# One list schedule for softmax attention, experts and the gated delta net: layer 0 from its router on joins layer 1's plan

## What is computed

```python
xn = layernorm(x)
s  = softmax_attention(xn)          # 16 heads of 16, causal, scores / 4
g  = silu(moe(xn))                  # 8 experts, top 2: silu(xn w1) * (xn w2), then w3
x  = x + s * g                      # layer 0
xn = layernorm(x)
s  = gated_delta_net(xn)            # 16 key heads, 32 value heads, conv of 4 taps
g  = silu(moe1(xn))                 # 2 shared experts, 16 routed, top 2, gelu
x  = x + s * g                      # layer 1
```

## Time and profile before

| what | us |
|---|---|
| median of 3 runs (lowest, highest) | 1588.99 (1585.53, 1592.14) |
| the profiled execution, its own time | 1583.53 |
| span of its trace | 1581.8 |
| PE busy, share of the span | 1443.0, 91% |
| DVE busy, share | 1244.6, 79% |
| ACT busy, share | 973.3, 62% |
| POOL busy, share | 650.3, 41% |

### The profile page before, as it was taken

The page is one execution under the profiler, slowest core; times in us unless marked ns, Lnnn a source line. Parts: engine busy times, 40 slices in busy tenths (PEclk is TensorE's granted clock), DMA queues, the critical chain, the costliest instruction groups (busy, mean ns, idle before and its releaser), DMA issues.

```text
span 1581.8 us, 33450 instructions
## 1 busy us (share of the span) xinstructions
PE 1443.0 (91%) x12600; PEld 1169.3 (74%) x12600; DVE 1244.6 (79%) x2613; ACT 973.3 (62%) x2525; POOL 650.3 (41%) x778
## 2 busy tenths in 40 slices
PE   6998778698899999989999999998999999999995
PEld 3554323386788888878878888887888888888883
DVE  3457624558888988979999888998989988898883
ACT  2100243238777677857777867776777777777763
POOL 7010032245545444445454444545354444443323
PEclk9999877769999999999999999999999999999997
DMA  9940000102111111111101111101021111011000
GB/s 289 115 53 4 4 0 1 40 21 52 34 28 35 35 28 28 41 28 35 35 28 35 35 35 28 48 21 48 8 55 28 31 32 35 22 37 32 9 1 27
DMA packets 52744, 59.37 MB, mean 38 GB/s; under 512 B 5352, under 2 KB 45032, under 8 KB 52584
## 3 DMA queue, kind: packets, MB, share of 16 engines
q1 hardware_dynamic: 52584, 57.23, 15.6%
HBM read 51.71 MB, written 5.51 MB: 36 GB/s over the span
## 4 chain that ended last, share of the span: by engine, by line
PE 67%; DVE 16%; POOL 5%; ACT 4%; issue 3%; DMA 3%; SPq 0%; POOLq 0%; DVEq 0%; ACTq 0%
PE ps L815 16%; PE ps L1155 6%; PE ps L867 4%; PE ps L1029 3%; PE ps L1133 3%; DVE O L1538 3%; PE ps L1137 3%; DMA RC<-crow 3%; PE ps L1109 3%; PE ps L1110 2%; PE ps L1071 2%; PE ps L1061 2%; PE ps L1125 2%; PE ps L1074 2%; DVE yv L1406 2%
## 5 line engine op out<-in xcount | busy, mean ns | idle before, releaser
L1724 ACT ACTIVATE XY<-ps 128x512 f16<-128x512 f32 x384 | 216.5, 598 | 103.9 <-PE ps L1074 102.8
L1471 DVE TENSOR_TENSOR ZL<-ps,cst 128x256 f16<-128x256 f32 x384 | 152.2, 416 | 26.9 <-PE ps L1061 24.8
L1866 POOL TENSOR_TENSOR RC<-RC,dec 128x512 f32<-128x512 f32 x64 | 67.0, 1047 | 232.8 <-DMA RC<-crow 232.7
L1406 DVE SCALAR_TENSOR_TENSOR yv<-ps,cw,yv 128x511 f32<-128x511 f32 (+2 forms) x192 | 142.9, 745 | 4.5
L1538 DVE SCALAR_TENSOR_TENSOR O<-O,small,Z 128x128 f32<-128x128 f32 x256 | 125.4, 550 | 9.5 <-POOL small L1897 9.5
L1155 PE MATMUL ps<-WO,OGT 128*128 128x256 f32 x512 | 127.8, 393 | 2.1 <-ACT OGT L1763 0.8
L1071 PE MATMUL ps<-ZL,XY 128*128 128x64 f16 x1536 | 103.9, 193 | 2.8 <-DVE ZL L1471 2.6
L1071 PEld LDWEIGHTS ps<-ZL,XY 128*128 128x128 f16 x1536 | 83.1, 98 | 30.2 <-issue 12.6
L1155 PEld LDWEIGHTS ps<-WO,OGT 128*128 128x128 f32 x512 | 94.0, 194 | 14.2 <-issue 1.1
L1074 PE MATMUL ps<-XY,ZL 128*128 128x64 f16 x1536 | 103.2, 193 | 0.0
L1061 PE MATMUL ps<-XY,LT 128*128 128x64 f16 x1536 | 96.8, 193 | 3.4 <-DVE yv L1406 1.1
(11 more groups left out here) (261 smaller groups left out, 4592.9 us busy)
## 6 DMA issues: line engine op xcount, KB each, us to landing
RC<-crow SPq DMA_DIRECT2D x128, 128.0 KB, 3.9
WV<-in_WV SPq DMA_DIRECT2D x16, 512.0 KB, 3.7
WK<-in_WK SPq DMA_DIRECT2D x16, 256.0 KB, 2.8
WO<-in_WO SPq DMA_DIRECT2D x16, 256.0 KB, 2.8
KS<-spread SPq DMA_DIRECT2D x6, 512.0 KB, 17.9
QS<-spread SPq DMA_DIRECT2D x6, 512.0 KB, 42.1
up<-in_up SPq DMA_DIRECT2D x18, 128.0 KB, 2.3
dn_w<-in_down SPq DMA_DIRECT2D x18, 128.0 KB, 2.4
```

The source lines that it names most:

```text
L1406: m = dve.scalar_tensor_tensor(out=dst[:, k:512], in0=ps[:, bk, 0:512 - k], scalar=cw[:, h, j, 3 - k:4 - k], in1=dst[:, k:512], op0=ALU.mu ...
L1471: leave(dve.tensor_tensor(half(ZL[:, k - 2], k, 0), p, lv(k), ALU.mult), "a", u, k)
L1724: leave(act.activation(changed(u, k), ps[:, bank("b", u, k), :].rearrange("p (c n t) -> p c n t", c=2, t=1 << (k - 1)), ACT.Copy), "b", u, k)
```

## The change

Layer 0 from the router on goes into the same plan as layer 1. `moe0`, `rows0`, the blend and both written orders are gone, and with them the barriers at `EXD_END`. Three new functions add the parts: `plan_experts0`, `plan_softmax0` and `plan_rows0`. `arrange` learns parts that take two neighbouring banks (`takes=2`). The arrival of QS and KS is a part on SP of 46 us (`stack`), the way of the maxima through DRAM one of 5 us (`max`).

The memory is laid out anew: w1 lies where XL comes later, and w2, w3, hT and the router's weights have room of their own beside PT and aT. So `ln1` (which writes XL) now comes after all expert products on PE, and nothing else in softmax waits for the experts but `op` on DVE, which needs the gate. The denominators are three items in place of one: `oc` (ACT), `ov` (PE, then DVE), `am` (POOL), each placed by itself. All eight XH copies of `ln1` are ACT's (before, DVE did four). What needs the new layernorm in layer 1 depends on `NEXT`, the last `ln1`. The numbers in `RANK` are other ones throughout, those of layer 1's parts too. No product, activation or DMA is added or left out.

```diff
--- before
+++ after
-ORDER_MOE0 = list(order_moe0())
-ORDER_SOFT0 = list(order_soft0())
...
+STEPS = [(b, g, j) for b in range(2) for g in range(4) for j in range(4)]
+STEP = {x: n for n, x in enumerate(STEPS)}
+PV_AT = {x: n + 1 for n, x in enumerate(x for x in STEPS if x[2] != 3)}
...
+            if p.takes == 2:
+                return min(((max(bank_at[b], bank_at[b + 1]), b) for b in spare if b % 2 == 0 and b + 1 in spare),
+                           default=None)
+            return min(((bank_at[b], b) for b in spare), default=None)
...
+def plan_experts0(P):
+    P.add(("rt",), -160, ("PE", 3.6), ("DVE", 0.3), takes=True, gives=("rt",))
+    P.add(("tp", 1), -160, ("DVE", 3.3, (("rt",), "DVE")), ("ACT", 1.5))
+    P.add(("tp", 2), -160, ("DVE", 3.0, (("tp", 1), "ACT")))
+    for k in range(16):
+        e, b = divmod(k, 2)
+        rank = -100 + 2 * k
+        old = [(("exd", *divmod(k - 3, 2), q), "PE") for q in range(2)] if k > 2 else []
+        x, y = ("exg", e, b), ("exv", e, b)
+        P.add(x, rank, ("PE", 1.72), ("ACT", 0.62, *old), takes=True, gives=x)
+        P.add(y, rank + 1, ("PE", 1.72), ("DVE", 0.69, (x, "ACT")), takes=True, gives=y)
+        for q in range(2):
+            z = "exd", e, b, q
+            P.add(z, rank + 2, ("PE", 0.86, (y, "DVE")), ("DVE", 0.96, (("exd", e - 1, b, q), "DVE") if e else (("tp", 2), "DVE")),
+                  takes=True, gives=z)
+    for b in range(2):
+        P.add(("g0", b), -60, ("ACT", 1.7, *[(("exd", 7, b, q), "DVE") for q in range(2)], (("g0", 0), "ACT") if b else None))
+
+
+def plan_softmax0(P):
+    P.add(("stack",), -300, ("SP", 46.0))
+    for b in range(2):
+        for g in range(8):
+            for i in range(4):
+                x = "p1", b, g, i
+                P.add(x, -200 + 20 * b, ("PE", 0.16 + 0.055 * (i + 1), (("stack",), "SP")),
+                      ("DVE", 0.1 + 0.27 * (i + 1)), takes=2, gives=x)
+        P.add(("tn0", b), -200 + 20 * b,
+              ("DVE", 0.7, *[(("p1", b, g, i), "DVE") for g in range(8) for i in range(4)], (("tn0", 0), "DVE") if b else None))
+        P.add(("tn", b), -200 + 20 * b, ("PE", 0.44, (("tn0", b), "DVE")), ("DVE", 0.68), takes=True, gives=("tn", b))
+        P.add(("max", b), -200 + 20 * b, ("SP", 5.0, (("tn", b), "DVE")))
+    for n, x in enumerate(STEPS):
+        b, g, j = x
+        part, no, rank = (4 - j) / 4, 4 * b + g, -190 + 80 * b + n % 16
+        back = STEPS[n - 3] if n > 2 else None
+        for k in range(2):
+            before = ("sc", *x, 0) if k else ("sc", *STEPS[n - 1], 1) if n else None
+            P.add(("sc", *x, k), rank, ("PE", 0.24 * part + 0.02, (("max", b), "SP"), before and (before, "PE")),
+                  ("ACT", 0.2 + 0.83 * part, back and (("pv", *back), "PE"), before and (before, "ACT")), takes=2,
+                  gives=("sc", *x, k))
+        last = ("pv", *STEPS[n - 1]) if n else None
+        P.add(("mk", *x), rank, ("POOL", 0.65, (("sc", *x, 0), "ACT"), (("sc", *x, 1), "ACT")))
+        P.add(("pv", *x), rank, ("PE", 0.86 * part + 0.05, (("mk", *x), "POOL"), last and (last, "PE")), takes=j == 0)
+        if j == 3:
+            am = (("am", *divmod(no - 2, 4)), "POOL") if no > 1 else None
+            P.add(("oc", b, g), rank, ("ACT", 0.62, (("pv", *x), "PE"), am), gives=("pv", b, g, 0))
+            P.add(("ov", b, g), rank, ("PE", 0.86, (("oc", b, g), "ACT")), ("DVE", 3.36, am), takes=True, gives=("ov", b, g))
+            P.add(("am", b, g), rank, ("POOL", 1.27, (("ov", b, g), "DVE")))
+
+
+def plan_rows0(P):
+    for n in range(NT):
+        b = n // 4
+        P.add(("op", n), -90 + 60 * b, ("PE", 1.72, *[(("am", b, g), "POOL") for g in range(4)]),
+              ("DVE", 1.2, (("g0", b), "ACT"), (("op", n - 1), "DVE") if n else None), takes=True, gives=("op", n))
+    for b in range(2):
+        P.add(("nrm", b), -90 + 60 * b, ("DVE", 2.0, *[(("op", n), "DVE") for n in range(4 * b, 4 * b + 4)],
+                                         (("nr2", 0), "DVE") if b else None), ("POOL", 1.3))
+        P.add(("nr2", b), -90 + 60 * b, ("DVE", 1.9, (("nrm", b), "POOL")))
+    experts = [((w, *divmod(k, 2)), "PE") for w in ("exg", "exv") for k in range(16)]
+    for n in range(NT):
+        b = n // 4
+        old = [(("ln1", n - 1), e) for e in ("PE", "ACT", "DVE")] if n else [None] * 3
+        P.add(("ln1", n), -90 + 60 * b, ("PE", 0.22, (("nr2", b), "DVE"), *experts, old[0]),
+              ("ACT", 0.4, old[1]), ("DVE", 0.42, old[2]), takes=True, gives=("ln1", n))
+    P.add(("spg",), -100, ("POOL", 1.0))
+    for h in range(2):
+        P.add(("fWK", h), -100, ("POOL", 1.9))
+    end = ("op", NT - 1), "DVE"
+    for h in range(2):
+        P.add(("fWV", h), -8 + 4 * h, ("SP", 4.5, end), ("POOL", 3.8))
+        P.add(("fWO", h), -6 + 4 * h, ("SP", 3.0, end), ("POOL", 0.7))
+        P.add(("fup", h), -7 + 4 * h, ("SP", 3.0, end), ("POOL", 1.0))
+    P.add(("cc", 1), -9, ("POOL", 0.6, end))
+    P.add(("cc", 2), -8, ("POOL", 4.5, (("cc", 1), "POOL")))
+    P.add(("cc", 3), -7, ("POOL", 1.5, (("cc", 2), "POOL"), (("ln1", NT - 1), "PE")))
+
+
+NEXT = ("ln1", NT - 1), "DVE"
...
-    P.add(("rt1",), -9, ("PE", 5.4), ("DVE", 0.3), takes=True, gives=("rt1",))
-    P.add(("wab",), -9, ("PE", 5.4), takes=True)
+    P.add(("rt1",), -9, ("PE", 5.4, NEXT), ("DVE", 0.3), takes=True, gives=("rt1",))
+    P.add(("wab",), -9, ("PE", 5.4, NEXT), takes=True)
...
-    for h in range(2):
-        P.add(("fWV", h), -8 + 4 * h, ("POOL", 3.8))
-        P.add(("fup", h), -7 + 4 * h, ("POOL", 1.0))
-        P.add(("fWK", h), -20 + h, ("POOL", 0.01))
+    plan_experts0(P)
+    plan_softmax0(P)
+    plan_rows0(P)
...
+        x0 = ExitStack()
+        w1 = sb("w1", [128, 2, 8, 128], scope=x0)
+        x0.close()
...
+        rw = sb("rw", [128, 2, 8], scope=sc)
+        w2 = sb("w2", [128, 2, 8, 128], scope=sc)
+        w3 = sb("w3", [128, 8, D], scope=sc)
+        hT0 = sb("hT", [128, 3, 512], scope=sc)
...
+            for x in ORDER1["PE"]:
+                what = x[0]
+                if what in ("rt1", "wab", "ck", "cq", "cv", "Zt", "up"):
+                    for n in range(NT):
+                        w.wait_ge(*done("ln1", n))
...
+                elif what == "oc":
...
+                    w.wait_ge(*full("pv", b, g, 0))
+                    if 4 * b + g > 1:
+                        w.wait_ge(s_aT, 4 * b + g - 1)
+                    leave(act.activation(OT[:, g % 2, :], ps[:, bank("pv", b, g, 0), :], ACT.Copy), "pv", b, g, 0)
...
```

539 lines of the change are left out of this document (217 added, 322 removed), and 10 rows, old and new, of the table RANK.

## The result

The changed kernel takes 1532.28 us in the median of 4 runs (1529.01 to 1534.32), against 1587.91 (1585.53 to 1592.14) for the kernel before on the same chip: a ratio of 0.9645, 95% interval 0.9617 to 0.9673. That is 55.6 us less, where 67.5 were forecast; the time lies inside the range, 11 us above the forecast. The profiled execution took 1534.32 us, its span is 1532.6.

A forecast was written before the change was run, and what follows sets the result against it. Layer 0's softmax was taken as a chain of handovers with no engine full. The steps ended layer 0 at 251.6 instead of 319.1 us, 67.5 less, giving 1521 us on the median's level; range 1496 to 1550.

The forecast's parts named there:

- The bound now: Layer 0's softmax, 189.1 to 294.5 us: no engine full, a chain of handovers, 12.5 us a group.
- Rival (a): Softmax period stays 12.5 us where no experts are left; step 5 takes 50 us, time 1539; chance 0.18.
- Step 1: Start of the row maxima: at 92 us instead of 104.5, with 7.9 half-experts remaining.
- Step 2: First batch's maxima: 40 us, 92 to 132, with 4.3 half-experts beside them.
- Step 3: Maxima's way through DRAM: 7 us, hidden behind experts; first batch's softmax starts at 139.
- step 4: Second batch's maxima with first batch's softmax: PE binds, 55 us to 187; second batch's softmax starts at 194.
- step 5: Second batch's softmax: four groups at 8 us each, 32 us, ending at 226.
- Step 6: Tail from softmax's last product to `rt1`: unchanged at 24.6 us, ending at 250.6.
- Step 7: ACT's silu/exp table loads: 0 to 12 loads, mostly hidden; 1 us added, 15 kept for the range.
- Step 9: Layer 1: same instructions, new ranks; change taken as 0, with 15 us either way for the range.
- Rival (c): Layer 1 gets slower by more than layer 0 gains, through its new order: 1600 and more; chance 0.04.
- Rival (b): The merge is limited by PE's work alone, 140 us from 92 on; layer 0 ends at 244, time 1502; chance 0.12.

The follow-up runs named there:

- E9: The kernel before, with ACT's copy of a group's sums two exps earlier for seven of eight groups: 1576.88 us, ratio 0.9927.
- E2: The changed kernel with ACT's silu of layer 0 replaced by a plain copy, removing the silu/exp table loads: 1527.85 us, ratio 0.9616.
- E10: The changed kernel with row maxima holding at most two bank pairs, root ahead of constants, layer 1's order held: 1527.10 us, ratio 0.9605.
- E12: E6 with half of the gate and value products of experts 4 to 7 left out: 1518.44 us, ratio 0.9566.
- E6: The changed kernel with POOL's layernorm root ahead of layer 1's casts, layer 1's order held: 1528.87 us, ratio 0.9627.
- E5: The kernel before, with only the changed kernel's RANK numbers for layer 1's parts: 1570.34 us, ratio 0.9886.
- E4: The changed kernel replanned with POOL's constants for layer 1 after the layernorm root, which also reordered layer 1: 1543.38 us, ratio 0.9713.
- E7: E6 with at most two bank pairs for maxima and the second batch's maxima ranked ahead of the first softmax: 1530.11 us, ratio 0.9629.
- E8: The changed kernel with one added 512-column bf16 product for each of the 64 row maxima: 1532.94 us, ratio 0.9649.
- E13: E10 with 30 added 512-column bf16 products on PE in the gap where it waits for the layernorm: 1519.90 us, ratio 0.9571.

## Why the prediction was right, and where it was off

**The bound now: right, in the main.** The handovers were a large part of the cost of softmax (E9 shows that the wait for the copy was one of them), and the plan removed most of them. The period was read from one group: 12.5 is the shortest of before but for its last, they go up to 15.0. After, the second batch's copies lie 11.9, 8.2 and 11.5 us apart, where 7 to 9 was forecast: the first with an expert and output rows on a PE that never rests (11.92 of 11.92 us), the last with 3.9 us of idle PE, 2.5 of it through the two table loads (E2). Rival (a), 12.5 where no experts are left at a clock of 0.7 to 0.8, didn't come: these three ran at 1.00, 1.00 and 0.88.

**Step 1: right.** First maxima at 92.8 us, forecast 92; half-experts left 7.8 (60 of 128 gate and value products at two thirds, 68 of 128 `exd` at one), forecast 7.9.

**Step 2: wrong in its order, right in what mattered least.** 30 us in place of 40, with less than one half-expert in place of 4.3. I had read that the plan's short costs would put more experts in than fit; it was the other way round, four pairs of banks shut them out. E10 prices that at some 2 us.

**Step 3: right.** MT was cast at 125.3, first exp at 133.1: 8 us on the way with PE's and ACT's turns, 7 forecast (133.1 is ahead of the 139 since step 2 was shorter).

**Steps 4 and 5: the step that failed.** The second batch's maxima were on their way into QS at 191.5, in time for the forecast 194. But PE and ACT were then still at the first batch's last group, with some three half-experts to come (last silu at 212.9). So the second batch's softmax began at 206.3, 12.3 us late (step 4), and took 49.9 in place of 32 us (step 5): in it PE was busy 45.65 us, with products of one and two thirds half-experts that I had put at none. The sum of PE's work is where the 30 us are. From 92 us to the last `pv` at 256.2 PE was busy 156.6 us and idle 7.6. Its groups sum to 175.6 us, overlaps included; scaled by 156.6 / 175.6 = 0.89, and with the half clock's 14.6 us taken out (13.0 scaled), the work at full clock is, as an estimate that takes one scale for all groups: maxima 44.8 x 0.89 = 40 (forecast 36), softmax groups (24.8 + 24.3 + 7.5) x 0.89 = 50 (49), experts (29.7 + 18.5) x 0.89 = 43 (41), the rest 10 (7): 143 where my terms made 133. So of the 30.2 us: 10 are prices too low by 2 to 11% and some 3 us of turns (`tn`, `ln1`) that had no term, 13 are the half clock, also without a term, and 7 or 8 are idle time. These sizes rest on rows; what a run confirms is that PE's work sets the end, for seven tenths (E12). One cause of the prices is in the timeline after, PE at 196 us:

```profile
196.21 1.98 PE L875 MATMUL ps<-xnT,w 128*128 128x512 f32 x4
198.12 0.45 PE L914 MATMUL ps<-QS,KS 64*128 64x384 f32 x2
...
```

Gate and value products each take 1.91 us from start to start, where two in a row take 3.43, 1.72 each, from 84.62 to the w3 products behind them before:

```profile
88.05 1.89 PE L875 MATMUL ps<-w,hT 128*128 128x256 f32 x8
```

I priced the half-experts by rows in which nothing else stood between them, and the change puts something between all of them. And I had written that the clock would stay above 0.9 from 92 to 190 us. It is 0.50 from 107 to 127, with PE busy 19.93 of 20 us.

**Step 6: 28.2 in place of 24.6.** POOL's casts ahead of the root are 2.4 of the 3.6 us (E6). I had asked what each engine has queued for the layernorm on PE and DVE, not on POOL.

**Step 7: more loads, and more than the 1 us taken.** 17 where I had 0 to 12; some 3.4 us (E2's 4.9 at `rt1` less the 1.5 it was ahead before any load counted) where I took 1 and kept 15. 2.5 of it are the gate's last pair, which stood in step 5 and not among the experts of step 4.

**Step 9: inside the 15 us, but not by chance of phase.** E5 shows that the new ranks alone bring 12 of the 14.5 us (16.8 in the median), and E4 that another order of layer 1 can cost as much. Rival (c) had the mechanism, the order, and the wrong sign.

**The sum.** Layer 0: 67.5 forecast, 34.7 measured; layer 1: 0 and 14.5. The forecast of 1521 held to 11 us because misses partly cancel: layer 0 gave 32.8 us less, layer 1 14.5 more, and the median moved by 6.4 more than the profiled spans. That is luck in good part. Without the 16.8 us of the ranks (E5) the time would be an estimated 1549, at the very edge of the range. Rival (b), PE's work as the bound, was nearest to what happened (E7 refutes the second batch's start as the limit, E12 confirms PE's work for seven tenths); its price, 140 us from 92 on, was too low by the same items.

## What to carry to other kernels

When a merge removes handovers, the end is set by the work of the engine that then never rests: price each piece of it as it will stand among other kinds, and ask in which stretches the clock will be granted, before trusting prices from pure stretches. A list scheduler that may give all banks to one kind of part will do so at the first tie; but look for what the freed time meets before mending it. And any edit of a greedy plan's costs, ranks or dependencies re-orders everything behind it, here by up to 12 us either way: hold the rest of the order fixed when you measure an edit, and try a few orders when you are done. Know how far a mark in one trace moves between executions of the same order, here 4 us, before you give a meaning to less. And a table load costs next to nothing while the engines have other work queued, and its full time where the last chain waits for it.

## What the runs showed of the hardware that I had not expected

- PE's granted clock was 0.50 over a stretch in which PE was shown busy 15.93 of 16 us, with scores of 64 rows and short bf16 products alone. One more bf16 product of 512 columns for each maximum held it at 1.00 (E8). In E13 small products of 16 columns began at full pace (0.11 us apart) and went on at half of it (0.21) from 281.0 us, 3 us later, with no gap between them.
- A table load took 1283 ns each time, and the next activation, where its input was there, started 1.29 us after the load did (201.83 after 200.54, 203.74 after 202.45).
- The same order of the same work, run twice, had a granted clock of 0.96 and of 0.84 between 145 and 189 us (before, E9), and was 4.3 us apart by then.
- A two-chunk product of 512 columns cost PE 1.91 us from start to start with another kind of product behind it, and 1.72 among its like.
